# Two groups of four heads in one PSUM bank, at two column offsets of V, in both attentions of a two-layer network

## The chip, the cores and the metric

The kernel runs on one core of one Trainium2 chip, as one program for the whole network. The metric is the device time of one execution in microseconds (us). The kernel before took 1137.66 us (median of three).

## What is computed

The input is x of shape 8 x 512 x 128 in float32: eight batches of 512 tokens. Four blocks follow one another, each with its residual and a layer norm:

```
x = layernorm(x + attention0(x))   # 16 heads of 8 dims, softmax(q k^T / sqrt(128)) v
x = layernorm(x + moe(x))          # router, 32 experts, top 6, and a shared expert
x = layernorm(x + attention1(x))   # rms norms, rotary q and k, sigmoid(q k^T / sqrt(8)),
                                   #   each row divided by its sum, then an output product
x = layernorm(x + ffn(x))          # silu(gate) * up, 384 hidden
```

The change touches the two attentions alone: the product of the weights with V, and the division by the row sums.

## The kernel before

**Layout.** P is 128, a batch (b, of NB = 8) has T = 512 tokens in NT = 4 tiles of 128. The 16 heads have HD = 8 dims and form NG = 4 groups of HG = 4 heads. A batch is walked in NU = 32 units u. In unit u TensorE (PE) makes two matmuls of transposed scores (`s2`, L528 in attention 0, L1217 in attention 1) into one of two PSUM buffers `ps_s`, and ScalarE (ACT) turns them into `prob` by one activation of 128 x 1024 elements (L404, L1162). In each odd unit follows `pv` (L541, L1230): four matmuls, one for each head of the group, which add the product with V into the bank `ps_o`. Head j of a group takes PSUM partitions 32j to 32j+31 (CT = 32). Its stationary operand is 32 columns of V: 8 of V, a column of ones (which yields the row sum) and 23 columns of zeros. A group is complete after four `pv`, that is eight units.

**After each group.** ACT copies the bank `ps_o` to `osb` (`take_o`, L376 in attention 0, where one of the two buffers is called moe_dsb; L1150 in attention 1), after which PE may start the next group. PE then turns it by four transposes (`turn_o`, L549, L1245), so that tokens lie on partitions, and VectorE (DVE) makes the reciprocals of the row sums and multiplies (`divide`: L614 and L617; in attention 1 first an addition, L1362, then L1364 and L1367). Four copies, four times four transposes and four divisions stand in a batch of either attention. The four results fill `att`, which then gets x added and is normalised.

**Attention 0** also needs the maximum of each score row for the softmax. For that PE makes the untransposed scores in 64 matmuls a batch (`s1`, L463), one for each n from 0 to 63, and DVE reduces each to a maximum (`reduce_max`, L605, TENSOR_REDUCE of 128 x 512). Two n belong to each unit. These tiles rotate through FB = 3 PSUM banks `ps_f`, and so do the guests: the products for q, k and v, the two turned sets of maxima (`max0`, `max1`) and the turned outputs o0 to o3. The list `TURNS` holds all of them in order, each guest before the n that `GUEST_AT` gives it (o0, o1, o2, o3 before n = 29, 46, 62, 9), and `BANK` gives turn number i the bank i % 3. `free_bank` makes PE wait until the turn that last used the bank has been read: by DVE for an n or an o, by ACT for q, k, v, max0 and max1. Three turns lie between two uses of a bank, except where the list starts again: with 73 turns the turn of n = 0 has bank 0, and so has the last one, n = 63, directly before it. The stretch that is reduced at n = 8 to 63 belongs to the next batch.

**Attention 1** has no maxima. Its PE also makes, between the units, the transposes and products for a later batch (`front_use` at units 18, 20, 22, 24, 26, 28: L1200, then L1204 to L1206), V of the next batch (unit 2, L1183), and for the batch before the transposes of `att` (`turn_all`, unit 6, L1252), the output product (`project`, unit 8, L1259) and the transposes of x (`turn_x_next`, unit 15, L1268). `turn_o` stands at units 4, 12, 20 and 28, `take_o` at units 1, 9, 17 and 25. DVE runs `divide` at 4, 12, 20 and 28, and in unit 20 right after it the two passes L1330 and L1332, for whose result (`xrl`) the products of unit 22 wait.

**Order.** Each engine's order is written by hand in its function `units`, called by `walk`; the middle six batches run in a loop of two batches a pass. The last division of each attention is done in the first steps of the stage that follows (`FirstOutput`, `LastOutput`).

## Time and profile before

| | us |
|---|---|
| median of three runs | 1137.66 |
| lowest and highest | 1135.06 and 1138.14 |
| the profiled execution's own time | 1139.23 |
| span of its instructions in the trace | 1137.4 |
| attention 0, start of the first to start of the last softmax pass | 62 to 449 |
| mixture of experts | 454 to 757 |
| attention 1, start of the first to start of the last sigmoid | 760 to 1059 |

The profiled execution is 1.57 us longer than the median. Its span is the time from the first to the last instruction, 1.8 us less than its time. In the rows below, a row of the timeline stands for one or several like instructions in succession, and gives what ended the engine's idle time before them where there was any. "PEld" is the loading of the stationary operand, which overlaps PE's matmuls. A duration in a group of such instructions is that of one; the engine often starts the next before the one ends, so that the distance between two starts is what an instruction costs its engine.

### The profile page before, as it was taken

What the parts mean: (1) busy time and instruction counts of PE and PEld (TensorE: products, weight loads), DVE (VectorE), ACT (ScalarE), POOL (GpSimd) and SP (SyncE); (2) the same over time, 40 slices, a digit from 0 to 9 for tenths busy, and PEclk for the clock granted to TensorE, in tenths of its full rate; (3) what the DMA queues carried; (4) which work ended last, traced back from release to release, by engine and by line L of the source; (5) the groups of instructions that cost most, each with busy time, mean ns of one, the idle gap of its engine ahead of it and who ended that gap; (6) DMA issues with size and microseconds to landing.
All of it is one profiled execution on the core that took longest, in us unless ns stands there. A gap on an engine that the chain in (4) does not pass through costs nothing. (4 is left out here: it accounts for less than half of the span.)

```text
span 1137.4 us, 20713 instructions
## 1 busy us (share of the span) xinstructions
PE 1049.2 (92%) x5936; PEld 497.3 (44%) x5936; DVE 819.1 (72%) x1919; ACT 753.4 (66%) x977; POOL 458.5 (40%) x464
## 2 busy tenths in 40 slices
PE   3989999999999798999999999989999999999796
PEld 1112222222222133788888887753333333322484
DVE  4878999999999884887888788855445544534466
ACT  0057777777777577555555555557888888899553
POOL 0313224132242432666777677664333133300265
PEclk9999999999999899999999999999999999999898
DMA  4463122231222000443324332533421233120011
GB/s 149 134 211 96 51 77 80 66 96 44 79 79 57 1 3 4 148 141 118 95 100 148 125 107 90 161 101 98 125 89 53 82 111 95 43 84 1 1 29 46
DMA packets 74078, 97.16 MB, mean 85 GB/s; under 512 B 12701, under 2 KB 42269, under 8 KB 73629
## 3 DMA queue, kind: packets, MB, share of 16 engines
q1 hardware_dynamic: 74024, 96.51, 27.2%
q8 instruction: 26, 0.43, 0.2%
q14 instruction: 28, 0.22, 0.1%
HBM read 68.29 MB, written 27.79 MB: 84 GB/s over the span
## 5 line engine op out<-in xcount | busy, mean ns | idle before, releaser
L605 DVE TENSOR_REDUCE a_nmax<-a_ps_f 128x1 f32<-128x512 f32 x512 | 322.3, 683 | 46.5 <-PE a_ps_f L463 43.0
L404 ACT ACTIVATE a_prob<-a_ps_s 128x1024 f32<-128x1024 f32 x256 | 252.7, 1023 | 93.3 <-PE a_ps_s L528 91.7
L1162 ACT ACTIVATE a_prob<-a_ps_s 128x1024 f32<-128x1024 f32 x256 | 249.0, 1033 | 37.9 <-PE a_ps_s L1217 35.1
L1990 POOL TENSOR_TENSOR moe_hl<-moe_hid,moe_hh 128x512 fp32r<-128x512 f32 x136 | 175.8, 1298 | 93.1 <-ACT moe_hh L1880 93.1
L463 PE MATMUL a_ps_f<-a_ks,a_qs 48*128 48x512 bf16 x512 | 178.1, 417 | 35.2 <-DVE a_nmax L605 16.1
L1870 ACT ACTIVATE moe_ps<-moe_ps 128x512 f32<-128x512 f32 x128 | 74.5, 582 | 118.8 <-PE moe_ps L1800 118.1
L463 PEld LDWEIGHTS a_ps_f<-a_ks,a_qs 48*128 48x128 bf16 x512 | 40.3, 94 | 239.6 <-DVE a_nmax L605 197.7
L541 PE MATMUL a_ps_o<-a_prob,a_va 128*32 128x512 f32 x1024 | 138.8, 615 | 0.1
L1230 PE MATMUL a_ps_o<-a_prob,a_va 128*32 128x512 f32 x1024 | 136.4, 605 | 2.5 <-ACT a_osb L1150 1.3
L528 PE MATMUL a_ps_s<-a_qs,a_ks 51*128 51x512 bf16 x512 | 135.3, 390 | 1.5 <-ACT a_prob L404 1.5
L1920 DVE TENSOR_TENSOR moe_prod<-moe_cw,moe_ps 128x512 f32<-128x512 f32 x128 | 87.3, 682 | 32.1 <-PE moe_ps L1800 29.2
L1217 PE MATMUL a_ps_s<-a_qs,a_ks 48*128 48x512 bf16 x512 | 94.2, 385 | 8.1 <-ACT a_prob L1162 5.4
L212 POOL TENSOR_TENSOR a_parts<-a_qk,g_zero 128x512 bf16<-128x512 f32 x28 | 29.1, 1038 | 156.8 <-DVE a_qk L1343 60.9
L1929 DVE TENSOR_TENSOR moe_hid<-moe_prod,moe_ps 128x512 f32<-128x512 f32 x128 | 87.0, 679 | 6.8 <-DVE moe_prod L1920 2.4
L1880 ACT ACTIVATE moe_hh<-moe_hid 128x512 fp32r<-128x512 f32 x136 | 84.8, 625 | 4.1 <-DVE moe_hid L1929 4.0
L1217 PEld LDWEIGHTS a_ps_s<-a_qs,a_ks 48*128 48x128 bf16 x512 | 23.6, 92 | 128.4 <-ACT a_prob L1162 81.5
L661 POOL TENSOR_TENSOR a_msplit<-a_nmax,g_zero 128x32 bf16<-128x32 f32 x16 | 3.8, 238 | 166.2 <-DVE a_nmax L605 166.2
L1798 PE MATMUL moe_ps<-moe_xh,moe_whig 128*128 (+1 forms) x136 | 55.7, 409 | 1.7 <-DVE moe_hid L1929 1.7
L1820 PE MATMUL moe_ps<-moe_hl,moe_whid 128*128 128x512 f32 x136 | 54.1, 398 | 0.8 <-POOL moe_hl L1990 0.8
L1817 PE MATMUL moe_ps<-moe_hh,moe_whid 128*128 128x512 f32 x136 | 54.1, 398 | 0.3 <-ACT moe_dsb L1888 0.3
L1799 PE MATMUL moe_ps<-moe_xh,moe_wlou 128*128 (+1 forms) x136 | 54.2, 398 | 0.0
L174 POOL TENSOR_TENSOR a_ve<-a_mv,g_eps 128x4 f32<-128x4 f32 x16 | 3.2, 201 | 126.4 <-DVE a_mv L146 126.4
(282 smaller groups left out, 1734.5 us busy)
## 6 DMA issues: line engine op xcount, KB each, us to landing
moe_cw<-r_weights SPq DMA_DIRECT2D x256, 128.0 KB, 2.9
parts_q<-a_parts SPq DMA_DIRECT2D x48, 256.0 KB, 2.5
parts_k<-a_parts SPq DMA_DIRECT2D x48, 256.0 KB, 2.5
a_qs<-parts_q SPq DMA_DIRECT2D x128, 96.0 KB, 2.4
a_ks<-parts_k SPq DMA_DIRECT2D x128, 96.0 KB, 2.5
a_xt<-in_x_t SPq DMA_DIRECT2D x8, 256.0 KB, 2.9
out_x<-g_X SPq DMA_DIRECT2D x8, 256.0 KB, 2.3
moe_wg<-in_wg SPq DMA_DIRECT2D x1, 1088.0 KB, 6.4
```

The costliest lines, as they stand in the source:

```text
L404: nc.scalar.activation(prob[:, u % PSLOTS, :, :], ps_s[:, u % 2, :, :], ACT.Exp, scale=float(P) ** -0.5).then_inc(exp_done, 1)
L463: nc.tensor.matmul(ps_f[:, bank, :], stack_rows(qs[p], h, QKR)[:, qt * P:(qt + 1) * P], stack_rows(ks[p], h, QKR), start=True, stop=True). ...
L528: mm = nc.tensor.matmul(ps_s[:, u % 2, i, :], stack_rows(ks[p], h, MXR)[:, kt * P:(kt + 1) * P], stack_rows(qs[p], h, MXR), start=True, st ...
L541: mm = nc.tensor.matmul(ps_o[j * CT:(j + 1) * CT, :], va[p][:, kt, grp * HG + j, :], prob[:, (2 * e + j // UN) % PSLOTS, j % UN, :], start ...
L605: nc.vector.tensor_reduce(nmax[:, half_no, h % 2, col:col + 1], ps_f[:, bank, :], AX.X, ALU.max, negate=True).then_inc(max_done, 1)
L1162: nc.scalar.activation(prob[:, u % PSLOTS, :, :], ps_s[:, u % 2, :, :], ACT.Sigmoid, scale=float(HD) ** -0.5).then_inc(exp_done, 1)
L1217: mm = nc.tensor.matmul(ps_s[:, u % 2, i, :], stack_rows(ks[p], h, QKR)[:, kt * P:(kt + 1) * P], stack_rows(qs[p], h, QKR), start=True, st ...
L1230: mm = nc.tensor.matmul(ps_o[j * CT:(j + 1) * CT, :], va[p][:, kt, grp * HG + j, :], prob[:, (2 * e + j // UN) % PSLOTS, j % UN, :], start ...
L1880: nc.scalar.activation(hh[:, part_at(j), :], hid[:, hid_at(j), :], ACT.Copy).then_inc(hh_done, 1)
L1920: nc.vector.tensor_tensor(prod[:, bank(j), :], cw[:, j % RC, :], ps_u[:, bank(j), :], ALU.mult).then_inc(prod_done, 1)
L1929: nc.vector.tensor_tensor(hid[:, hid_at(j), :], prod[:, bank(j), :], ps_g[:, bank(j), :], ALU.mult).then_inc(hid_done, 1)
L1990: nc.gpsimd.tensor_tensor(hl[:, part_at(j), :], hid[:, hid_at(j), :], hh[:, part_at(j), :], ALU.subtract).then_inc(hl_done, 1)
```

## The change

Two groups now share the bank `ps_o`. `PER_O` = 2 groups make one output, `NO` = 2 outputs a batch, and `SLOT` = 16 is the distance between the two groups on the partitions of a head. The buffer `va` gets 16 columns of zeros at its front. For the first group of a pair the 32 stationary columns start at the head's own place (8 of V, ones, zeros), for the second they start 16 columns earlier (16 zeros, then 8 of V, ones, zeros). The rows 32j to 32j+15 of the bank thus hold a head of the first group, the rows 32j+16 to 32j+31 one of the second, and each adds zeros to the other. The accumulation starts at every eighth `pv` and stops seven later.

The core of the diff:

```diff
-OT_AT = (29, 46, 62, 9)
+OT_AT = (46, 9)
...
+def v_of_head(flat, kt, h):
+
+    at = (kt * H + h) * CT + SLOT * (h // HG % PER_O == 0)
+    return flat[:, at:at + CT]
...
+def output_parts(ps):
+
+    return ps.rearrange("p (k j q c) -> p k j q c", k=NT, j=HG, q=PER_O)
...
+def divide_outputs(nc, att, n, o, rec, done):
+
+    to, spread = outputs_of(att, n), [P, NT, HG, HD]
+    for q in range(PER_O):
+        ins = nc.vector.tensor_tensor(to[:, :, :, q, :], o[:, :, :, q, 0:HD],
+                                      rec[:, :, :, q].unsqueeze(3).broadcast_to(spread), ALU.mult)
+    ins.then_inc(done, 1)
...
-                        if second and u % 8 == 1 and (back if u > 8 else tail):
-                            take_o(*((b, u // 8 - 1) if u > 8 else (b - 1, NG - 1)))
+                        if second and u % 16 == 1 and (back if u > 16 else tail):
+                            take_o(*((b, u // 16 - 1) if u > 16 else (b - 1, NO - 1)))
...
-                if kt == 0:
-                    pe.wait_ge(o_taken, NG * b + grp + O_C)
+                if e % (PER_O * NT) == 0:
+                    pe.wait_ge(o_taken, NO * b + grp // PER_O + O_C)
...
-                                          start=(kt == 0), stop=(kt == NT - 1))
+                                          start=(e % (PER_O * NT) == 0), stop=((e + 1) % (PER_O * NT) == 0))
...
-                nc.vector.memset(va[i][:, :, :, HD + 1:CT], 0.0).then_inc(cleared, 1)
-                nc.vector.memset(va[i][:, :, :, HD:HD + 1], 1.0).then_inc(cleared, 1)
+                nc.vector.memset(v_tiles(va[i])[:, :, :, HD + 1:CT], 0.0)
+                nc.vector.memset(va[i][:, 0:SLOT], 0.0).then_inc(cleared, 1)
+                nc.vector.memset(v_tiles(va[i])[:, :, :, HD:HD + 1], 1.0).then_inc(cleared, 1)
...
-                    if u % 8 == TURN_AT and (back if u > 8 else tail):
-                        turn_o(*((b, u // 8 - 1) if u > 8 else (b - 1, NG - 1)))
+                    if u % 16 == TURN_AT and (back if u > 16 else tail):
+                        turn_o(*((b, u // 16 - 1) if u > 16 else (b - 1, NO - 1)))
```

So the copies at units 9 and 25, the transposes and divisions at units 12 and 28 (attention 1) and the guests before n = 29 and n = 62 (attention 0) are gone; those at units 1 and 17, 4 and 20, n = 46 and n = 9 stay where they were. The list of turns has 71 entries: n = 0 now follows the last user of its bank, n = 62, by two places, n = 1 follows n = 63 by two, and n = 2 follows n = 61 by five. Everywhere else three turns lie between two uses, as before. In attention 1 the transposes of x (unit 15) now wait for `y_taken`, the sum read by DVE at unit 8, instead of the first division of the batch. `turn_o` for the pair at unit 20 waits for `x_parted`, as the second group did before.

What stands on DVE in attention 0, from the first `divide` of the batch before the last to the first steps of the last batch; this part is written out without a loop. Before (L605 is `reduce_max`, L614 and L617 are `divide`):

```order
L605 TENSOR_REDUCE a_nmax<-a_ps_f 128x1 x5
L614 RECIPROCAL a_rec<-a_ps_f 128x16
L617 TENSOR_TENSOR moe_y<-a_ps_f,a_rec 128x4x32
L605 TENSOR_REDUCE a_nmax<-a_ps_f 128x1 x17
L614 RECIPROCAL a_rec<-a_ps_f 128x16
L617 TENSOR_TENSOR moe_y<-a_ps_f,a_rec 128x4x32
L605 TENSOR_REDUCE a_nmax<-a_ps_f 128x1 x16
L614 RECIPROCAL a_rec<-a_ps_f 128x16
L617 TENSOR_TENSOR moe_y<-a_ps_f,a_rec 128x4x32
L605 TENSOR_REDUCE a_nmax<-a_ps_f 128x1 x10
```

and now (L641 is `reduce_max`, L650 the reciprocal, L208 the two products):

```order
L641 TENSOR_REDUCE a_nmax<-a_ps_f 128x1 x22
L650 RECIPROCAL a_rec<-a_ps_f 128x32
L208 TENSOR_TENSOR moe_y<-a_ps_f,a_rec 128x4x32 x2
L641 TENSOR_REDUCE a_nmax<-a_ps_f 128x1 x26
L650 RECIPROCAL a_rec<-a_ps_f 128x32
```

The first and the third division are gone, the two that stay have a reciprocal of twice the elements and two products of the old size.

On ACT at the end of attention 1, from the copy for the batch before the last to the last one; L1162 is the sigmoid, L1150 `take_o`. Before:

```order
L1150 ACTIVATE a_osb<-a_ps_o 128x512
L1162 ACTIVATE a_prob<-a_ps_s 128x1024 x8
L1150 ACTIVATE a_osb<-a_ps_o 128x512
L1162 ACTIVATE a_prob<-a_ps_s 128x1024 x8
L1150 ACTIVATE a_osb<-a_ps_o 128x512
L1162 ACTIVATE a_prob<-a_ps_s 128x1024 x6
L1150 ACTIVATE a_osb<-a_ps_o 128x512
```

and now (L1193 is the sigmoid, L1181 the copy):

```order
L1181 ACTIVATE a_osb<-a_ps_o 128x512
L1193 ACTIVATE a_prob<-a_ps_s 128x1024 x16
L1181 ACTIVATE a_osb<-a_ps_o 128x512
L1193 ACTIVATE a_prob<-a_ps_s 128x1024 x14
L1181 ACTIVATE a_osb<-a_ps_o 128x512
```

Every second copy is gone, and sixteen sigmoids stand between two copies.

On DVE at unit 20 of attention 1, in the loop (L1350 scales x, L1391 to L208 are `divide`, L1359 and L1361 make the two halves of the scaled x for the products of unit 22), now:

```order
L1350 TENSOR_TENSOR a_xr<-a_xb,a_rr 128x512
L1390 ISA
L1391 TENSOR_SCALAR a_rec<-a_ps_t 128x32
L1392 ISA
L1393 RECIPROCAL a_rec<-a_rec 128x32
L1394 REGISTER_ALU
L208 TENSOR_TENSOR a_att<-a_ps_t,a_rec 128x4x32 x2
L1354 REGISTER_ALU
L1359 CAST a_xrh<-a_ps_f 128x512
L1361 TENSOR_TENSOR a_xrl<-a_ps_f,a_xrh 128x512
```

The order is that of before; the division ahead of the two passes has become longer.

## Rows read from the trace of the kernel before

**Rows 1.** Windows: us, busy time of each engine, PEclk, DMA share and GB/s
```profile
106.00:350.00 244.00, 232.01 (x1477) 63.47 (x1469) 225.80 (x436) 183.49 (x212) 65.81 (x95) 1.00 0.25 75
818.80:1042.90 224.10, 214.75 (x1490) 72.85 (x1487) 102.01 (x273) 197.98 (x217) 56.32 (x57) 1.00 0.23 71
```

**Rows 2.** Timeline of DVE, attention 0: start, us, instruction, [idle before, releaser]
```profile
197.38 0.25 DVE L614 RECIPROCAL a_rec<-a_ps_f 128x16 f32<-128x16 f32 x1
197.66 0.29 DVE L617 TENSOR_TENSOR moe_y<-a_ps_f,a_rec 128x128 f32<-128x128 f32 x1
197.87 3.44 DVE L605 TENSOR_REDUCE a_nmax<-a_ps_f 128x1 f32<-128x512 f32 x5
201.94 6.86 DVE L605 TENSOR_REDUCE a_nmax<-a_ps_f 128x1 f32<-128x512 f32 x11 [0.62 <-PE a_ps_f L463]
...
211.16 4.27 DVE L605 TENSOR_REDUCE a_nmax<-a_ps_f 128x1 f32<-128x512 f32 x7 [0.48 <-PE a_ps_f L463]
```

**Rows 3.** Timeline of DVE, attention 0: after `max1`, and three batches on
```profile
218.71 3.18 DVE L605 TENSOR_REDUCE a_nmax<-a_ps_f 128x1 f32<-128x512 f32 x5 [0.29 <-PE a_ps_f L463]
...
339.79 0.25 DVE L614 RECIPROCAL a_rec<-a_ps_f 128x16 f32<-128x16 f32 x1
```

**Rows 4.** Groups by line: count, busy us, mean ns, idle before and releaser
```profile
L614 DVE RECIPROCAL a_rec<-a_ps_f 128x16 f32<-128x16 f32 x31 | 7.7, 249 | 3.0 <-PE a_ps_f L549 2.8
L1625 DVE RECIPROCAL r_score<-r_e 128x128 f32<-128x128 f32 x8 | 7.5, 941 | 0.0
```

**Rows 5.** Timeline of PE, attention 0, before n = 0
```profile
208.57 1.06 PE L541 MATMUL a_ps_o<-a_prob,a_va 128*32 128x512 f32 x8
...
210.74 0.39 PE L463 MATMUL a_ps_f<-a_ks,a_qs 48*128 48x512 bf16 x2 [0.57 <-DVE a_nmax L605]
```

**Rows 6.** Weight loads of L1268: duration ns min, median, max, first and last start
```profile
L1268 PEld LDWEIGHTS a_ps_t<-g_ident,a_xb x28: 138/140/143, 818.8 to 1042.9; 128*128 128x128 f32 x28
```

**Rows 7.** Timeline of ACT, attention 1, one batch
```profile
927.39 0.60 ACT L1150 ACTIVATE a_osb<-a_ps_o 128x512 f32<-128x512 f32 x1
927.88 5.83 ACT L1162 ACTIVATE a_prob<-a_ps_s 128x1024 f32<-128x1024 f32 x6
934.13 1.94 ACT L1162 ACTIVATE a_prob<-a_ps_s 128x1024 f32<-128x1024 f32 x2 [0.42 <-PE a_ps_s L1217]
...
949.22 1.02 ACT L1162 ACTIVATE a_prob<-a_ps_s 128x1024 f32<-128x1024 f32 x1 [0.37 <-PE a_ps_s L1217]
```

**Rows 8.** Timeline of PE, attention 1, the same batch
```profile
922.62 0.66 PE L1252 MATMUL a_ps_t<-g_ident,a_att 128*128 128x128 f32 x4
...
928.04 1.07 PE L1230 MATMUL a_ps_o<-a_prob,a_va 128*32 128x512 f32 x8 [0.18 <-ACT a_osb L1150]
...
929.36 0.66 PE L1245 MATMUL a_ps_t<-g_ident,a_osb 128*128 128x128 f32 x4
929.94 0.39 PE L1217 MATMUL a_ps_s<-a_qs,a_ks 48*128 48x512 bf16 x2
...
941.41 0.50 PE L1204 MATMUL a_ps_f<-a_xrh,a_wh 128*128 128x512 f32 x1
```

**Rows 9.** Timeline of DVE, attention 1: divisions at units 4 and 20
```profile
921.57 0.29 DVE L1367 TENSOR_TENSOR a_att<-a_ps_t,a_rec 128x128 f32<-128x128 f32 x1
...
939.04 0.17 DVE L1362 TENSOR_SCALAR a_rec<-a_ps_t 128x16 f32<-128x16 f32 x1
...
940.60 0.69 DVE L1332 TENSOR_TENSOR a_xrl<-a_ps_f,a_xrh 128x512 fp32r<-128x512 f32 x1
```

**Rows 10.** Timeline of ACT, last batch of attention 1
```profile
1045.97 7.61 ACT L1162 ACTIVATE a_prob<-a_ps_s 128x1024 f32<-128x1024 f32 x8
```

**Rows 11.** Timeline of DVE, start of the kernel
```profile
4.35 0.11 DVE L597 MEMSET a_va<- 128x64 f32 x1
```

**Rows 12.** Windows at the one stall of PE in attention 0
```profile
369.50:377.00 7.50, 0.48 (x3) 0.00 (x0) 7.50 (x6) 1.02 (x1) 5.91 (x2) 0.73 0.00 0
377.00:382.00 5.00, 4.74 (x19) 0.91 (x20) 3.35 (x7) 1.26 (x2) 0.00 (x0) 0.50 0.00 0
```

**Rows 13.** Timeline of PE right behind that stall
```profile
378.83 1.93 PE L541 MATMUL a_ps_o<-a_prob,a_va 128*32 128x512 f32 x8
```

More of the change, by code:

```diff
@@ L24 @@
 CT = P // HG
+PER_O = 2
+NO = NG // PER_O
+SLOT = CT // PER_O
 PARTS = 3
@@ L1163, in units @@
                                              scale=float(HD) ** -0.5).then_inc(exp_done, 1)
-                    if u % 8 == 1 and (back if u > 8 else tail):
-                        take_o(*((b, u // 8 - 1) if u > 8 else (b - 1, NG - 1)))
+                    if u % 16 == 1 and (back if u > 16 else tail):
+                        take_o(*((b, u // 16 - 1) if u > 16 else (b - 1, NO - 1)))
             act.sem_inc(exp_done, EXP_C)
@@ L1409, in units @@
                         take_v(b + 1, 1 - p)
-                    if u % 8 == TURN_AT and (back if u > 8 else tail):
-                        divide(*((b, u // 8 - 1) if u > 8 else (b - 1, NG - 1)))
+                    if u % 16 == TURN_AT and (back if u > 16 else tail):
+                        divide(*((b, u // 16 - 1) if u > 16 else (b - 1, NO - 1)))
                     if back and is_last(b) and u in FFN_W_AT:
@@ L1493, in tensor @@
         if k == 1:
-            pe.wait_ge(self.att_done, NG * NB + 1)
+            pe.wait_ge(self.att_done, NO * NB + 1)
             for kt in range(NT):
```

173 lines of the change are left out of this document (84 added, 89 removed).

## The prediction

> **What bounds the kernel now.** I read the windows first, over a steady stretch of each attention. In attention 0 DVE is busy for 225.8 of 244 us, and ACT for 183.5; in attention 1 ACT is busy for 198.0 of 224.1 us and DVE for only 102.0 [rows 1]. PE shows 232.0 and 214.8 us, but a busy PE is modelled, so the timelines must decide. In attention 0 they say DVE: eleven reductions in 6.86 us stand without a gap, 0.62 us each, and what gaps there are end with an `s1` tile of PE [rows 2]. A batch lasts (339.79 - 197.38) / 3 = 47.5 us [rows 2, 3], and its 64 reductions take some 40 of them. In attention 1 a batch lasts (1042.9 - 818.8) / 6 = 37.35 us [rows 6], with two modes inside it. Where PE has only units to do, ACT runs six sigmoids in a row in 5.83 us [rows 7]: ACT bounds. Where PE has transposes or products in between, ACT waits 0.37 to 0.42 us for the scores [rows 7]: PE bounds. So three engines have to be followed, and the same edit is worth something else in each place. The mixture of experts and the last stage contain nothing of the change but its two heads.
>
> **Attention 0, per batch.** (a) Two of four divisions go. One costs DVE the time from 197.38 to 197.87, 0.49 us [rows 2], and DVE is the bound: 2 x 0.49 = 0.98 gained. The transposes that go with them (PE) and the copies (ACT) lie beside it and count nothing more. (b) The two that stay get longer. The reciprocal has 32 elements instead of 16: between 16 elements in 249 ns and 128 in 941 ns the slope is (941 - 249) / 112 = 6.2 ns [rows 4], so 0.10 us more. There is one more product, 0.21 us from start to start (197.66 to 197.87) [rows 2]. Together 0.31, twice: 0.62 lost. (c) But behind both stand gaps in which DVE waits for PE: 0.62 us behind the one at n = 46 [rows 2], and 0.29 behind the one at n = 9 [rows 3]. PE goes on while DVE divides longer, so part of the 0.62 falls into them. The bounds are 0 (PE is held by the three banks and gains no lead) and 0.62 (PE uses all of it, the second gap lacking 0.02); I take the middle, 0.3. (d) The list starts again without a bank that is used twice in succession. Before, PE waits 0.57 us for the reduction of n = 63 before it may make n = 0 [rows 5], and DVE then idles 0.48 [rows 2]. With two places between them, PE can make n = 0 while DVE reduces n = 63, which takes 0.62 and so is longer than the 0.48 of the round trip. But PE is still held at n = 1 until n = 63 is done, and the `pv` behind it (1.06 us, eight passes for its four matmuls [rows 5]) then comes later; a short gap may stand behind that. Bounds 0 and 0.48, I take 0.3, nearer to the full row since the round trip itself is hidden. Sum: 0.98 - 0.62 + 0.3 + 0.3 = 0.96 us a batch; from 0.36 to 1.46. Seven batches run with reductions and divisions together: 6.7 us (2.5 to 10.2).
>
> The last batch of attention 0 has no reductions; DVE, PE and ACT take turns there over the router's first steps. Two divisions go and one gets longer, 0.98 - 0.31 = 0.67 if all lies on the path, 0 if none. With PE's and ACT's parts the upper end is 1.2. I take 0.5.
>
> [...]
>
> **Attention 1, per batch.** (e) The copy at unit 9 stands in the stretch that ACT bounds: it costs from 927.39 to 927.88, 0.49 us [rows 7]. The `turn_o` that goes with it (unit 12) is hidden there, since PE waits for ACT anyway. (f) The copy at unit 25 and the `turn_o` of unit 28 stand where PE bounds: the transposes cost PE from 929.36 to 929.94, 0.58 us [rows 8], and ACT waits 0.37 behind such places [rows 7]; its copy is then free. Together 1.07. PE also waited 0.18 for the copy before the first `pv` of a group [rows 8]; that is the same time as the copy's and is counted only as an upper end, 1.25. (g) The division at unit 20 gets longer by 0.31, and by 0.02 for the addition over 32 elements. Behind it on DVE stand the two passes that make `xrl`, and for that PE's products of unit 22 wait: `xrl` ends at 941.29, and PE starts them at 941.41 [rows 8, 9], so there is 0.12 of slack and some latency; the delay is 0.2 to 0.33 where the division is the late one, and 0 where PE's own transposes of unit 20 are. I take 0.25 lost. (h) The division at unit 4 also gets longer, and `turn_all` waits for it: it ended at 921.86 and the transposes began at 922.62 [rows 8, 9], 0.76 us later. 0.33 fits in: nothing. Without that cover it would cost up to 0.33. (i) The new wait of unit 15 is for the sum of unit 8, which DVE made long before: nothing. Net 1.07 - 0.25 = 0.82 a batch; from 0.4 to 1.25. Seven batches: 5.7 us (2.8 to 8.7). The last batch has no fronts, ACT runs eight sigmoids in a row [rows 10], and two copies of 0.49 go: 1.0 (0.5 to 1.0).
>
> **Once only.** Two more short memsets on DVE at the start, each under the 0.11 of a 64-column one [rows 11], two on GpSimd, and 0.31 more in either head of the following stage, where PE and ACT have other work. I take 0.3 lost (0 to 0.8). No DMA is added, moved or passed; the matmuls of `pv` keep their number, shape and partitions, and read the same count of columns.
>
> **The sum.** 6.7 + 0.5 + 5.7 + 1.0 - 0.3 = 13.6 us, with ends of 5 and 21. The profiled execution took 1139.23, so a like one takes 1125.6; the median is 1.57 lower than it, 1137.66, so the forecast is **1124.0 us**.
>
> **The rivals.**
> *A, the new waits take most of it.* PE gains no lead in (c), the two short distances of (d) cost as much as the one they replace, and (g) costs its full 0.33 while DVE's and PE's parts in (e) and (f) only half show. Then attention 0 gives 0.36 x 7 = 2.5 and attention 1 0.4 x 7 + 0.5 = 3.3: about 6 us, 1131.7. For it speaks that gaps of 0.62 and 0.29 come from PE's bursts, which the change does not touch; against it, that the wait of 0.57 in rows 5 plainly hangs on a bank that the change frees. 0.16.
> *B, more is gained.* In attention 0 PE is nearly as full as DVE. With two transposing turns less PE gets 2 x 0.58 us of lead, and gaps behind the k product and `max0` (0.62 each) shrink; in attention 1 everything of (e) and (f) counts. Attention 0 gives 1.5 x 7, attention 1 1.15 x 7 + 1: 19 us, 1118.5. 0.16.
> [...]
> *D, within measurement of no change.* The time goes into waits that the rows do not show, of ACT for `pv` or of DVE for transposes: 1137.7. 0.04.
>
> **How the numbers follow.** The forecast has 0.60, A and B 0.16 each, C and D 0.04 each. The predicted time is the forecast's. From 1116 to 1133 the range takes in nearly all of the forecast's ends and most of A and B, and leaves out C and D. About 0.3%, or 3.4 us, is what a measurement of this kernel can tell from no change. Faster by more than that: the forecast, B, and nearly all of A, 0.89. Within it: D and the tail of A, 0.07. Slower: C, 0.04.
>
> **What would show it.** In the trace after: the idle 0.48 before n = 0 gone or under 0.2, batches of attention 0 of 46.5 us, a division of 0.80 us from start to the next reduction, a reciprocal of about 0.35 us. In attention 1 batches of 36.5 us, six or more sigmoids in a row without a copy, and `xrl` later than PE's wish for it by 0.2 or so at unit 22. PEclk of 1.00 in both stretches. The forecast is wrong if the batches of attention 0 stay at 47.1 or above, if PE idles before L1204 for more than 0.4, or if a granted clock under 1.00 shows in the steady stretches.

## The result, and the profile after

The changed kernel takes **1121.5 us** (median of four, 1118.78 to 1123.58), the kernel before 1137.9 in the same comparison. The ratio is 0.9854 with a 95% interval of 0.983 to 0.9878, so 13.9 to 19.3 us are gained. The forecast was 1124.0 in a range of 1116 to 1133. It held, but the sum is better than its terms: those of attention 0 and of the start were too small, those of attention 1 too large, and one stage that gained, the mixture of experts, stood nowhere in the sum. That these errors cancel is luck.

The profiled execution took 1123.58 us against 1139.23. The landmarks in both traces, in us:

| stretch | before | after | difference | forecast |
|---|---|---|---|---|
| start to the first exponential | 62.2 | 60.8 | -1.4 | +0.3 |
| attention 0, first to last exponential | 386.8 | 376.8 | -10.0 | -7.2 |
| from there to the first sigmoid of attention 1 | 311.4 | 309.9 | -1.5 | 0 |
| attention 1, first to last sigmoid | 298.3 | 295.4 | -2.9 | -6.7 |
| from there to the end | 78.7 | 78.6 | -0.1 | 0 |

Two of these differences hold more than the change. Attention 1 of the kernel before takes 298.3 us here, but 299.3 in two kernels of the experiments with the same code for it (e1, e6). At its start the clock's record differs: before, PEclk is 1.00 from 458 to 1062 us, and after there is a stretch at 0.50 from 746.0 to 752.9. Here is PE from 746 to 753 us in the changed kernel and then in e12, which has the same attention 1 and no such stretch:

```profile
746.00:753.00 7.00, 6.14 (x26) 0.51 0.28 85
```

```profile
746.00:753.00 7.00, 5.53 (x40) 1.00 0.28 85
```

Between kernels that agree in this, attention 1 gains 3.9 us both ways: 299.3 (e1) to 295.4 (after) with the stretch at 0.50, 298.3 (before) to 294.3 (e12) without it. So 2.9 is too low for the change by 1.0. The other difference is that of the mixture of experts; it is taken up under "Sixty-four bytes".

**The steady stretches.** First the windows, with the columns of [rows 1] (PE, PEld, DVE, ACT, POOL, PEclk, DMA share, GB/s), then the weight loads that answer to [rows 6] and the group that answers to [rows 4].

```profile
120.00:350.00 230.00, 219.08 (x1390) 58.66 (x1382) 216.95 (x413) 173.00 (x196) 65.47 (x94) 1.00 0.25 75
806.00:1028.00 222.00, 209.92 (x1446) 68.08 (x1444) 98.68 (x249) 192.71 (x205) 56.36 (x57) 1.00 0.23 71
```

```profile
L1297 PEld LDWEIGHTS a_ps_t<-g_ident,a_xb x28: 137/141/143, 806.3 to 1027.7; 128*128 128x128 f32 x28
```

```profile
L650 DVE RECIPROCAL a_rec<-a_ps_f 128x32 f32<-128x32 f32 x12 | 4.2, 348 | 0.0
```

The granted clock is 1.00 in both stretches. The reciprocal of 32 elements takes 348 ns; that of 16 took 249 [rows 4], so 99 ns more, as worked out: it lies on the line through 16 and 128 elements (249 + 16 x 6.18 = 348).

**Attention 0 on DVE**, one batch (the timeline that answers to [rows 2] and [rows 3]):

```profile
146.69 0.35 DVE L650 RECIPROCAL a_rec<-a_ps_f 128x32 f32<-128x32 f32 x1
147.07 0.49 DVE L208 TENSOR_TENSOR moe_y<-a_ps_f,a_rec 128x128 f32<-128x128 f32 x2
147.47 3.14 DVE L641 TENSOR_REDUCE a_nmax<-a_ps_f 128x1 f32<-128x512 f32 x5
151.24 9.95 DVE L641 TENSOR_REDUCE a_nmax<-a_ps_f 128x1 f32<-128x512 f32 x16 [0.62 <-PE a_ps_f L498]
161.48 3.78 DVE L641 TENSOR_REDUCE a_nmax<-a_ps_f 128x1 f32<-128x512 f32 x6 [0.30 <-PE a_ps_f L498]
165.17 0.35 DVE L650 RECIPROCAL a_rec<-a_ps_f 128x32 f32<-128x32 f32 x1
165.56 0.49 DVE L208 TENSOR_TENSOR moe_y<-a_ps_f,a_rec 128x128 f32<-128x128 f32 x2
165.96 4.46 DVE L641 TENSOR_REDUCE a_nmax<-a_ps_f 128x1 f32<-128x512 f32 x7
...
192.84 0.35 DVE L650 RECIPROCAL a_rec<-a_ps_f 128x32 f32<-128x32 f32 x1
```

From 146.69 to 192.84 a batch takes 46.15 us; the next ones alternate between 46.07 and 46.15, mean 46.11. Before it was 47.47. Segment by segment:

- From the division at n = 46 to the end of the wait behind it: 197.38 to 201.94 before, 4.56 us [rows 2]; 146.69 to 151.24 now, 4.55. The division is 0.29 longer and nothing came later: the five reductions behind it took 3.44 us [rows 2] and now take 3.14. They had short waits between them (the second began 0.11 us after the first had ended), and these are filled. The wait of 0.62 behind them is the same.
- From there to the division at n = 9 there are 22 reductions. Before, with a division and the 0.48 us of wait [rows 2], they took 201.94 to 216.65, 14.71 us; now 151.24 to 165.17, 13.93. The division is 0.49 of the 0.78. The wait of 0.48 before n = 0 is gone, but one of 0.30 has come a few turns later.
- Behind n = 9 the wait of 0.29 [rows 3] is gone: seven reductions follow without a gap. It has taken up the longer division.
- In the rest of the batch the fourth division went, 0.49. The wait before n = 26 is 0.43 where it was 0.34.

The four make 1.3 us. The pair of batches shown is a short one before and a long one after; by the means, a batch gains 1.36 to 1.38.

The wait of 0.30 comes from one of PE for a bank. PE may make n = 1 only when n = 63, two turns earlier in the same bank, has been reduced, and behind n = 1 and n = 2 stands a `pv`, so that n = 3 is late (timeline of PE, at n = 1):

```profile
159.45 0.39 PE L498 MATMUL a_ps_f<-a_ks,a_qs 48*128 48x512 bf16 x1 [0.31 <-DVE a_nmax L641]
```

**Attention 1 on ACT**, the batch that answers to [rows 7]:

```profile
912.74 1.02 ACT L1193 ACTIVATE a_prob<-a_ps_s 128x1024 f32<-128x1024 f32 x1 [0.31 <-PE a_ps_s L1248]
914.14 5.76 ACT L1193 ACTIVATE a_prob<-a_ps_s 128x1024 f32<-128x1024 f32 x6 [0.37 <-PE a_ps_s L1248]
920.38 1.94 ACT L1193 ACTIVATE a_prob<-a_ps_s 128x1024 f32<-128x1024 f32 x2 [0.49 <-PE a_ps_s L1248]
...
926.46 1.02 ACT L1193 ACTIVATE a_prob<-a_ps_s 128x1024 f32<-128x1024 f32 x1 [0.90 <-PE a_ps_s L1248]
927.86 1.02 ACT L1193 ACTIVATE a_prob<-a_ps_s 128x1024 f32<-128x1024 f32 x1 [0.37 <-PE a_ps_s L1248]
929.11 1.02 ACT L1193 ACTIVATE a_prob<-a_ps_s 128x1024 f32<-128x1024 f32 x1 [0.23 <-PE a_ps_s L1248]
```

The six sigmoids at 914.14 have no copy before them any more, but a wait of 0.37 us in its place. The sigmoid ahead of them is 912.74 now and 926.37 in the trace of before, 13.63 us apart; the six start at 914.14 and 927.88 [rows 7], 13.74 apart. The copy of 0.49 was worth 0.11. At 929.11 stands a wait of 0.23 that was not there.

PE shows why, in the same batch:

```profile
911.22 1.16 PE L1288 MATMUL a_ps_t<-a_w,a_att_t 128*128 128x128 f32 x8
912.31 0.39 PE L1248 MATMUL a_ps_s<-a_qs,a_ks 48*128 48x512 bf16 x2
912.63 1.07 PE L1261 MATMUL a_ps_o<-a_prob,a_va 128*32 128x512 f32 x8
913.63 0.61 PE L1248 MATMUL a_ps_s<-a_qs,a_ks 48*128 48x512 bf16 x4
```

The output product of unit 8 (L1288, 1.16 us) and a `pv` make the scores of unit 10 late; ACT would have waited for them without the copy too. The copy stood in a PE-bound place, one unit ahead of the ACT-bound stretch for which the prediction took it.

The turn at unit 28 that went cost PE 0.41 us, from 949.03 to 949.44, not the 0.58 of unit 12 in [rows 8]: here a matmul of products follows it, there the scores (timeline of PE, kernel before):

```profile
949.03 0.65 PE L1245 MATMUL a_ps_t<-g_ident,a_osb 128*128 128x128 f32 x4
949.44 0.48 PE L1204 MATMUL a_ps_f<-a_xrh,a_wh 128*128 128x512 f32 x1
```

From there to the next single pair of scores before and after drift apart by 0.38. In all: 0.11 + 0.38, less 0.11 at unit 22 (below), 0.38 a batch. A steady batch fell from 38.05 to 37.67 us. The mean of six intervals fell from 37.35 to 36.9 (806.3 to 1027.7), but one of the six, from unit 15 of the seventh batch to unit 15 of the last, has no fronts: 33.5, now 32.75.

**The start.** The timeline of DVE, before and then after, at the split of the first k:

```profile
12.17 0.43 DVE L211 CAST a_parts<-a_qk 128x512 bf16<-128x512 f32 x1 [0.48 <-ACT a_qk L376]
```

```profile
11.39 0.42 DVE L245 CAST a_parts<-a_qk 128x512 bf16<-128x512 f32 x1
```

With 73 turns q and k had the same bank, 0, and PE waited 2.05 us at the start until ACT had copied q. With 71 turns k has bank 2. The wait of 0.48 is gone. Over all runs with a trace, the first exponential starts at 62.2 to 62.3 us in the four kernels in which q and k share a bank, and at 60.6 to 61.3 in the ten in which they do not. The start of the first reduction (22.95 before, 22.25 now, but 22.8 in e1 and e12) also hangs on a DMA, that of the parts of k: ahead of its first scores PE waits for it 10.8 us in the kernel before, 12.7 in the changed one, 13.4 in e1 and 13.1 in e12. No run changed the bank of k alone.

### The profile page after: what moved, and what is told of

Its sections match the earlier page's. It is cut to its first block and busy times, and to the rows that moved or that the text cites. A ratio compares the mean times of both kernels' runs of the same rounds, so it can differ in the third digit from the quotient of the medians.

```text
span 1121.5 us, 20149 instructions
## 1 busy us (share of the span) xinstructions
PE 1032.1 (92%) x5808; PEld 485.4 (43%) x5808; DVE 811.5 (72%) x1873; ACT 737.4 (66%) x945; POOL 458.8 (41%) x466
## 5 line engine op out<-in xcount | busy, mean ns | idle before, releaser
L641 DVE TENSOR_REDUCE a_nmax<-a_ps_f 128x1 f32<-128x512 f32 x512 | 320.0, 684 | 41.0 <-PE a_ps_f L498 40.1
L1193 ACT ACTIVATE a_prob<-a_ps_s 128x1024 f32<-128x1024 f32 x256 | 248.9, 1029 | 42.9 <-PE a_ps_s L1248 40.0
L1895 ACT ACTIVATE moe_ps<-moe_ps 128x512 f32<-128x512 f32 x128 | 74.5, 582 | 117.4 <-PE moe_ps L1825 116.7
L1823 PE MATMUL moe_ps<-moe_xh,moe_whiu 128*128 (+1 forms) x136 | 54.0, 397 | 0.0
L1824 PE MATMUL moe_ps<-moe_xh,moe_wlog 128*128 (+1 forms) x136 | 53.8, 396 | 0.0
```

Source lines behind the costliest of these rows:

```text
L641: nc.vector.tensor_reduce(nmax[:, half_no, h % 2, col:col + 1], ps_f[:, bank, :], AX.X, ALU.max, negate=True).then_inc(max_done, 1)
L1193: nc.scalar.activation(prob[:, u % PSLOTS, :, :], ps_s[:, u % 2, :, :], ACT.Sigmoid, scale=float(HD) ** -0.5).then_inc(exp_done, 1)
L1823: nc.tensor.matmul(dst, w[0][:, j, :], hi, start=True, stop=False)
```

## The experiments

The times are medians, each beside runs of the kernel before on the same chip; a batch of attention 0 is the mean of two neighbours, one of attention 1 is a steady one, and the mixture of experts (MoE) is read from the first to the last of its 128 sigmoids on ACT (L1870, L1895), in the profiled execution.

| kernel | us | ratio, 95% interval | att. 0 batch | att. 1 batch | MoE |
|---|---|---|---|---|---|
| before | 1137.9 | 1 | 47.49 | 38.05 | 293.9 |
| after | 1121.5 | 0.9854 (0.983 to 0.9878) | 46.11 | 37.67 | 291.4 |
| e1, attention 0 alone | 1125.49 | 0.9878 (0.9852 to 0.9904) | 46.11 | 38.05 | 291.3 |
| e2, attention 1 alone | 1130.0 | 0.9923 (0.9904 to 0.9942) | 47.48 | 37.64 | 291.1 |
| e3b, +0.4 on DVE at n = 46 | 1122.17 | 0.9866 (0.9845 to 0.9887) | 46.11 | 37.67 | 292.5 |
| e4b, +0.4 on DVE at n = 9 | 1121.34 | 0.985 (0.9828 to 0.9871) | 46.38 | 37.67 | 292.7 |
| e5, after, 72 places | 1120.13 | 0.9835 (0.9813 to 0.9857) | 45.99 | 37.67 | 292.5 |
| e6, before, 74 places | 1136.67 | 0.9985 (0.9973 to 0.9997) | 47.48 | 38.05 | 293.9 |
| e7, copy at unit 9 | 1122.26 | 0.9864 (0.985 to 0.9879) | 46.10 | 37.69 | 291.6 |
| e9, division behind xrl | 1120.85 | 0.9845 (0.9823 to 0.9868) | 46.11 | 37.56 | 291.6 |
| e10, before, buffers 64 bytes lower | 1135.12 | 0.9966 (0.9955 to 0.9977) | 47.48 | 38.06 | 290.7 |
| e11, three findings together | 1118.14 | 0.9827 (0.9813 to 0.9842) | 45.99 | 37.50 | 291.7 |
| e12, after, MoE buffers back | 1121.92 | 0.9849 (0.9836 to 0.9861) | 46.11 | 37.67 | 291.1 |
| e13, e11 with banks from n = 16 | 1121.51 | 0.985 (0.9837 to 0.9863) | 46.11 | 37.50 | 292.5 |

The times differ less than their intervals for most pairs. The batches in the traces repeat to 0.02 us between kernels that share the code, so small terms are read from them. Spans of a whole stage do not: the MoE varies by 1.4 us between kernels with the same placement and the same code for it.

### Each attention alone

In e1 the function `attention1` and the class `LastOutput` are those of before, and the rest is as changed; in e2 it is the reverse, with the shift of the top buffers in both:

```diff
-        wide = nc.sbuf_usable_end // 32 * 32 - 2 * NB * T * 4
+        wide = nc.sbuf_usable_end // 32 * 32 - 2 * NB * T * 4 - SLOT * 4
```

> The change in attention 0 alone; attention 1 and its head as before. Theory T (read from the two traces): attention 0 gives 1.3 us in each of seven batches and about 2 more in its first and last, so 11 to 12 us: about 1126.5 against 1137.9, and batches of attention 1 stay at 37.35. Rival F (the split of the forecast): attention 0 gives 7.2, so about 1130.7. Rival N: the gains of the two attentions do not add, since less work in one changes what the other meets; then this and the kernel with the change in attention 1 alone sum to something other than 16.4.

> The change in attention 1 alone; attention 0 as before. Theory T: 0.45 us in each of seven batches and 0.5 to 1 in the last, so 3 to 4.5 us: about 1134, batches of attention 0 at 47.45, of attention 1 at 36.9. Rival F: 6.7 us, about 1131.2. With the kernel that changes attention 0 alone the gains sum to 15 to 17 us by T.

e1 gains 12.8 us by the medians, nearer to theory T than to the 7.2 of the forecast's split; its attention 0 takes 376.0 us, 10.8 less than before. e2 gains 8.3, far more than the 3 to 4.5 of T. But its trace shows only 3.9 of it in attention 1 (294.4 instead of 298.3 us from the first to the last sigmoid). Another 2.8 lie between the attentions, in the MoE, where neither change does anything. The two gains sum to 21.1, and the whole change gives 16.4. The intervals of the three are wide (some 3, 2 and 3 us to either side), but the traces say the same: something is in both halves and counts once. That is rival N in its outcome, though not by its reason, and it led to e10.

### A longer division

The edit of e3b (of e4b with `n == 1`, the division at n = 9):

```diff
                 divide_outputs(nc, att, n, o, rec, att_done)
+                if n == 0:
+                    nc.vector.memset(pad[:, :], 0.0)
```

> The changed kernel, with a memset of 400 columns of an unused tile on DVE behind the division at n = 46 of attention 0: about 0.4 us more of DVE work there in each of eight batches. Theory T: DVE's longer work there runs beside a burst of PE that sets the next reduction but four; DVE still waits 0.62 us behind it, that wait shrinks to 0.2 and batches stay at 46.15 (at most 0.1 longer, under 1 us in all). Rival D: the banks hold PE back as DVE is late, and the 0.4 counts in full: batches of 46.55, about 3 us more.

> The same behind the division at n = 9, where the changed kernel leaves no wait of DVE. Theory T: the change has used up the wait of 0.29 us there, so the 0.4 counts until the next wait for PE that no bank causes: 0.2 to 0.4 in each of seven batches, 1.5 to 2.9 us. Rival P: PE alone sets the length of a batch, the wait of 0.43 us behind n = 26 takes the 0.4, and the time moves by under 0.5 us.

The timeline of DVE in e3b, behind n = 46:

```profile
147.55 0.39 DVE L655 MEMSET a_pad<- 128x400 f32 x1
147.86 3.01 DVE L642 TENSOR_REDUCE a_nmax<-a_ps_f 128x1 f32<-128x512 f32 x5
151.20 9.94 DVE L642 TENSOR_REDUCE a_nmax<-a_ps_f 128x1 f32<-128x512 f32 x16 [0.33 <-PE a_ps_f L499]
```

The memset delays the five reductions by 0.43 us, the wait of 0.62 shrinks to 0.33, and the batch stays at 46.11. Theory T holds, rival D falls. In e4b a batch is 0.27 longer (46.38): between the ends that T gave, and not rival P. So the two places differ. Behind n = 46 DVE still waits for PE after the change, and 0.4 us more fits in. Behind n = 9 the change had used up the wait, and only 0.16 of the 0.43 still fits between the seven reductions, which take 4.30 instead of 4.46. The times cannot tell these differences; the batches do.

### The banks

The edit of e5 and of e6 is the same line:

```diff
-BANK = {t: i % FB for i, t in enumerate(TURNS)}
+BANK = {t: (i + (i >= TURNS.index(21))) % FB for i, t in enumerate(TURNS)}
```

> The changed kernel, with the three banks of attention 0 numbered one further from turn n = 21 on, so that the list has 72 places and starts again with each bank three turns old; the two short distances (two turns) now stand at n = 21 and 22, where DVE writes four products of the normalisation, 1.11 us, between two reductions. Theory T: the gap of 0.30 us some turns after the start of the list comes from the two-turn distances there and goes; nothing comes back at n = 21, since PE makes the two tiles beside the 1.11 us; batches of attention 0 go from 46.1 to 45.85, 2 us in all, about 1119.5. Rival P: that gap comes from PE's own burst of a pv and transposes and stays; the time does not move (within 0.5 us a run), or the gap only moves.

> The kernel before with nothing changed but the numbering of the banks, one further from n = 21 on: the list has 74 places, and it starts again with two turns between uses of a bank, as in the changed kernel, where it was one. Theory T (term (d) of the prediction, measured alone): the wait of PE of 0.57 us before n = 0 and DVE's 0.48 behind it go, 0.30 stay; a batch of attention 0 gets 0.2 to 0.35 shorter, 47.45 to 47.15, 2 us in all, about 1136. Rival P: the wait is only handed on to the next burst, and nothing is gained (47.4).

The timeline of DVE in e6, from the division at n = 62 on:

```profile
207.36 3.28 DVE L605 TENSOR_REDUCE a_nmax<-a_ps_f 128x1 f32<-128x512 f32 x5
210.94 3.77 DVE L605 TENSOR_REDUCE a_nmax<-a_ps_f 128x1 f32<-128x512 f32 x6 [0.30 <-PE a_ps_f L463]
...
227.55 1.89 DVE L605 TENSOR_REDUCE a_nmax<-a_ps_f 128x1 f32<-128x512 f32 x3 [0.57 <-PE a_ps_f L463]
```

Where the list starts again the wait of 0.48 is replaced by one of 0.30, as in the changed kernel. The eleven reductions from 207.36 to 214.63 take 7.27 us, and took 7.45 (209.20 to 216.65) before: 0.18 gained. But before n = 26 the wait is 0.57 where it was 0.34, since the short distances at n = 21 and 22 hold PE ahead of the q product. The batch is the same, 47.48. Rival P describes it: the wait was handed on, here by my own edit. The price of term (d) alone is thus 0.18 us where the list starts again; over a batch this edit shows nothing of it. The time of e6 is 0.15% below that of before (0.03 to 0.27%), about 1.7 us; of that the last batch of attention 0 holds 0.26 us (41.53 to 41.27), the steady ones nothing, and where the rest lies stays open.

In e5 the wait of 0.30 goes (22 reductions in a row) and the one before n = 26 grows from 0.43 to 0.57:

```profile
149.90 13.72 DVE L641 TENSOR_REDUCE a_nmax<-a_ps_f 128x1 f32<-128x512 f32 x22 [0.62 <-PE a_ps_f L498]
...
176.46 1.89 DVE L641 TENSOR_REDUCE a_nmax<-a_ps_f 128x1 f32<-128x512 f32 x3 [0.57 <-PE a_ps_f L498]
```

T had the cause of the 0.30 right, and was wrong that the short distances cost nothing at n = 21. Net 0.12 a batch, half of what T gave, and 0.8 us in seven batches.

### The copy of unit 9

```diff
+                    if u == 9 and tail:
+                        act.wait_ge(ot_done, NO * b + OT_C)
+                        nc.scalar.activation(osb[:, 1, :], osb[:, 1, :], ACT.Copy)
```

> The changed kernel with a copy on ScalarE (ACT) of a 128x512 tile put back at unit 9 of attention 1 in seven batches, without the transposes and the division that went with it (it copies a tile onto itself). Theory T: the copy stands in a wait of 0.37 us of ACT for the scores, which comes from the product with W_o that PE makes at unit 8; it costs 0.12 us a batch, under 1 us in all (a batch 36.9 to 37.0). Rival F (term (e) of the prediction): ACT is the bound there and the copy costs 0.49 us a batch, 3.4 us in all (37.4).

The timeline of ACT in e7, around unit 9:

```profile
913.48 1.02 ACT L1193 ACTIVATE a_prob<-a_ps_s 128x1024 f32<-128x1024 f32 x1 [0.31 <-PE a_ps_s L1251]
914.40 0.62 ACT L1199 ACTIVATE a_osb<-a_osb 128x512 f32<-128x512 f32 x1
914.92 5.75 ACT L1193 ACTIVATE a_prob<-a_ps_s 128x1024 f32<-128x1024 f32 x6
```

The copy takes the place of the wait of 0.37, and the six sigmoids start 1.44 us behind the one before them instead of 1.40. A batch is 0.02 to 0.04 longer, attention 1 in all 0.3 us. Theory T holds with an even lower price; term (e) of the prediction, 0.49, falls.

### The division ahead of xrl

The edit of e9 moves the division of unit 20 in DVE's program:

```diff
-                    if u % 16 == TURN_AT and (back if u > 16 else tail):
-                        divide(*((b, u // 16 - 1) if u > 16 else (b - 1, NO - 1)))
+                    if u == TURN_AT and tail:
+                        divide(b - 1, NO - 1)
...
                     if u in FRONT_AT and qk_on:
                         take_front(b + 2, p, FRONT_AT.index(u))
+                    if u == 16 + TURN_AT and back:
+                        divide(b, 0)
```

> The changed kernel, with the division of unit 20 of attention 1 placed behind the two passes that make xrh and xrl on DVE, not ahead of them. Theory T (term (g) measured): xrl is made 0.2 us earlier against PE's transposes, PE's products of unit 22 no longer wait for it, and the wait of ACT of 0.23 us behind them goes: 0.1 to 0.2 us a batch, about 1 us in all (a batch 36.75; xrl ends at least 0.15 us earlier after the transposes than in the changed kernel). Rival F (the size in the prediction): 0.25 a batch and 1.8 us. Rival X: PE's transposes of unit 20 are what is late, since they wait 0.58 us for xr, and nothing moves (36.9).

The timeline of ACT behind it has no wait of 0.23 any more:

```profile
927.57 1.02 ACT L1193 ACTIVATE a_prob<-a_ps_s 128x1024 f32<-128x1024 f32 x1 [0.90 <-PE a_ps_s L1248]
928.97 2.17 ACT L1193 ACTIVATE a_prob<-a_ps_s 128x1024 f32<-128x1024 f32 x2 [0.37 <-PE a_ps_s L1248]
```

A batch takes 37.56 instead of 37.67: term (g) is 0.11 us, by removing it alone. T holds. Where the rest of the 0.33 went, the first of the two passes (`xrh`) shows, against PE's transposes of unit 20, before and then after:

```profile
939.18 0.66 PE L1200 MATMUL a_ps_f<-g_ident,a_xr 128*128 128x128 f32 x4 [0.58 <-DVE a_xr L1321]
...
939.88 0.69 DVE L1330 CAST a_xrh<-a_ps_f 128x512 fp32r<-128x512 f32 x1
```

```profile
925.44 0.65 PE L1231 MATMUL a_ps_f<-g_ident,a_xr 128*128 128x128 f32 x4 [0.58 <-DVE a_xr L1350]
...
926.32 0.68 DVE L1359 CAST a_xrh<-a_ps_f 128x512 fp32r<-128x512 f32 x1
```

Before, the pass began 0.04 us after the transposes had ended (939.84): they were the late ones, and not the division. Now it begins 0.18 later against them (0.88 us from their start instead of 0.70), so 0.15 of the 0.33 is hidden behind the transposes, and 0.06 of the rest in the slack before PE's products. The 0.7 us that this makes in all is less than the interval of the times.

### Sixty-four bytes

The row of V is 16 columns longer in the changed kernel, and to make room for it the buffers at the top of SBUF start 64 bytes lower. In the MoE those addresses hold `moe_xh` and `moe_xl`, the moving operands of six of nine products. The edit of e10, in the kernel before:

```diff
-        wide = nc.sbuf_usable_end // 32 * 32 - 2 * NB * T * 4
+        wide = nc.sbuf_usable_end // 32 * 32 - 2 * NB * T * 4 - 64
```

> The kernel before, with nothing changed but the place of the buffers at the top of SBUF, 64 bytes lower, as the change puts them; in the mixture of experts these are the moving operands of two thirds of the products. Theory S: the matmuls that read them are some ns shorter each, the stage's 128 units take 291.2 us from the first to the last sigmoid instead of 293.9, and the time falls by 2 to 4 us, to about 1135. It would explain why the gains of the two halves, 12.8 and 8.3, add up to more than the 16.8 of both. Rival I: the place of the instructions, not of the data, makes the difference, or chance does; then the stage stays at 293.9 and the time at 1137.9.

e12 is the changed kernel with the MoE's two buffers, and the first stacks of attention 1 that lie in the same place, put back:

```diff
-        e[name] = nc.alloc_sbuf_tensor_at("a1_" + name, [P, HH, T], BF16, offset=wide + i * NB * T * 4)
+        e[name] = nc.alloc_sbuf_tensor_at("a1_" + name, [P, HH, T], BF16, offset=wide + 64 + i * NB * T * 4)
...
-            m["xh"], m["xl"] = (nc.alloc_sbuf_tensor_at(f"moe_x{n}", [P, NB, T], F32R, offset=wide + i * NB * T * 4)
+            m["xh"], m["xl"] = (nc.alloc_sbuf_tensor_at(f"moe_x{n}", [P, NB, T], F32R, offset=wide + 64 + i * NB * T * 4)
```

> The changed kernel with the buffers at the top of SBUF that the mixture of experts reads (its two halves of x, and the first stacks of attention 1 that lie in the same place) put back 64 bytes, to where they were before; those of attention 0 stay 64 bytes lower. Theory S: the stage's products take some ns more each again, its 128 units take 293.9 us instead of 291.4, and the time rises by 2 to 3 us, to about 1124; both attentions stay as they are (46.1 us a batch, and 37.7). Rival O: the address that matters is another one (of attention 0's tiles or of what follows them), and nothing moves (291.5, 1121.5).

The first and last of the MoE's sigmoids (line, count, ns min/median/max, first and last start), in the order before, after, e10, e12:

```profile
L1870 ACT ACTIVATE moe_ps<-moe_ps x128: 582/582/591, 455.4 to 749.3; 128x512 f32<-128x512 f32 x128
```

```profile
L1895 ACT ACTIVATE moe_ps<-moe_ps x128: 582/582/593, 444.8 to 736.2; 128x512 f32<-128x512 f32 x128
```

```profile
L1870 ACT ACTIVATE moe_ps<-moe_ps x128: 582/582/591, 456.0 to 746.7; 128x512 f32<-128x512 f32 x128
```

```profile
L1895 ACT ACTIVATE moe_ps<-moe_ps x128: 582/582/590, 444.5 to 735.6; 128x512 f32<-128x512 f32 x128
```

e10 is 0.34% faster than the kernel before (0.23 to 0.45%), with not one instruction changed, and its MoE takes 290.7 us instead of 293.9. Not all of this is the placement. The first sixteen units of the stage take 36.8 to 38.1 us, and differ by up to 1.3 between kernels with the same code and the same placement; the clock's record falls to 0.50 for 3 to 7 us near their start in all traces but that of e12. From the 17th sigmoid to the last it is 256.1 us before and 253.5 in e10: the place of data matters by 2.5 us. Theory S as it stood falls with e12, though: with the MoE's buffers back where they were the stage does not return to 293.9 but takes 291.1. It is not the address of these buffers by itself.

Between the 17th and the 97th sigmoid, a stretch that repeats best, the fourteen traces show three levels: 182.33 and 182.46 (before, e6); 180.66, 180.67 and 180.85 (e10, e2, e12); 181.28 to 181.38 (all nine others). What fits all of them, as a reading made afterwards: the change also makes `rec` of attention 0 64 bytes larger, and what is allocated behind it, the MoE's weights among it, moves up by 64. The distance between weights and x is then the old one in the first level, 64 bytes less in the second (by the one shift or by the other), and 128 less in the third. That it is the distance was not tried by itself, and why it should matter stays open. From the 17th sigmoid to the last the same three groups take 255.9 to 256.1, 253.5 to 253.8 and 254.5 to 254.6 us, so that 1.4 us of the change's gain go with the placement. The products agree with the grouping: over the whole stage the mean of that of `moe_hh` with `moe_wlod` is 394 ns before and 395 in e6, 388 in e10 and in e2, 389 in e12, and 396 after. e2 and e10 differ in their instructions and agree in these numbers; before and e10 have the same instructions and do not. So rival I, the place of the instructions, falls. One of the 80 units between those sigmoids takes 182.46 / 80 = 2.281 us before and 2.258 in e10, 1% less.

### Three findings together

e11 has the banks of e5, the division of e9, and the scores of unit 21 ahead of the transposes of xr, for which PE waits 0.58 us:

```diff
+                    if u == FRONT_AT[1] + 1 and qk_on:
+                        front_use(b + 2, p, 1, front)
...
-                    if u in FRONT_AT and qk_on:
+                    if u in FRONT_AT and qk_on and u != FRONT_AT[1]:
                         front_use(b + 2, p, FRONT_AT.index(u), front)
```

> A version built from the findings: the changed kernel with the banks renumbered from n = 21 on, the division of unit 20 behind xrl, and PE's scores of unit 21 placed ahead of the transposes of xr, which wait 0.58 us for DVE. Theory T: 3.1 us from the banks (from the trace of the kernel with that alone), 1 from the division, and 0.32 us a batch (2.2 in all) from the scores that fill PE's wait: 6.3 less than the changed kernel, about 1115.2; batches of attention 0 45.7, of attention 1 36.4 to 36.5. Rival X: the scores made earlier gain nothing, since ACT is given its next tile by the same burst; then 1117.4 and 36.75 a batch. Rival Y: the xr chain then becomes later and the 0.3 is lost in unit 22: 1119.

e13 is e11 with `TURNS.index(16)` in place of `TURNS.index(21)`.

> The version with all three findings, with the banks renumbered from n = 16 on and not from n = 21: there DVE makes the statistics of the normalisation, 1.2 us, between two reductions, and five more reductions and the normalisation lie between it and the q product. Theory T: the 0.14 us that the short distances at n = 21 cost before n = 26 (a wait of 0.57 instead of 0.43) is not paid at n = 16, since PE has more of DVE's other work to catch up beside: batches of attention 0 45.8 to 45.85 instead of 46.0, 1 us less than the version with n = 21, about 1117. Rival P: v's product or its copy by ACT is late instead, a wait stands behind n = 16 or the 0.57 stays, and batches stay at 46.0 or are longer.

e11 has the lowest median of all, 1118.14. Its ratio to before, 0.9827, overlaps with that of the changed kernel, 0.9854. Its trace supports 1.9 us of the 3.4: 0.12 in each of seven batches and 0.17 in each of six. The scores moved ahead gave only 0.06 of their 0.32 a batch. The timeline of PE says why: the wait for xr is 0.26 instead of 0.58, but the products of unit 22 now wait 0.19 for xrl. That is most of rival Y; the xr chain sets the pace there, and filling PE's wait only shows the next one. T had also put the banks at 3.1 us, the difference of the whole spans of attention 0 in after and e5 (376.8 and 373.8); the batches hold 0.8 of it, and e11, with the same banks, takes 375.8. The rest did not repeat.

```profile
923.98 0.66 PE L1231 MATMUL a_ps_f<-g_ident,a_xr 128*128 128x128 f32 x4 [0.26 <-DVE a_xr L1352]
...
926.14 0.50 PE L1235 MATMUL a_ps_f<-a_xrh,a_wh 128*128 128x512 f32 x1 [0.19 <-DVE a_xrl L1363]
```

e13 puts the short distances at n = 16. The wait before n = 26 is 0.43 again, as T had it, but one of 0.33 stands five turns earlier, and a batch takes 46.11: rival P.

```profile
174.04 1.29 DVE L641 TENSOR_REDUCE a_nmax<-a_ps_f 128x1 f32<-128x512 f32 x2 [0.33 <-PE a_ps_f L498]
...
178.58 1.89 DVE L641 TENSOR_REDUCE a_nmax<-a_ps_f 128x1 f32<-128x512 f32 x3 [0.43 <-PE a_ps_f L498]
```

The change in the banks is worth 0.12 us a batch at n = 21 and nothing at n = 16. A list of 71 turns over three banks has to have its short distances somewhere.

## Why the prediction was right, and where it was not

**(a) Two divisions of 0.49 us gone, 0.98 a batch.** Right; each shows whole, since DVE bounds around them.

**(b) The longer division, 0.62 for both.** Right as a size: 0.78 to 0.79 us from start to next reduction, 0.80 forecast; the reciprocal 348 ns, 0.35 forecast.

**(c) Half of it falls into gaps, 0.3.** This step was sized wrongly: all of it did, 0.6, the upper bound that the prediction gave. It took the middle between the bounds, for want of a row that says whether PE gains a lead, and it looked for the room in the wrong place behind n = 46: the gap of 0.62 stayed as it was. The trace had the row: the five reductions behind n = 46 took 3.44 us [rows 2], 0.69 each, where eleven others took 0.62 each. Such excess is waiting in short pieces that the timeline does not print, and it went when the division got longer. e3b shows that even 0.43 us more would have been hidden.

**(d) The start of the list, 0.3.** The effect is there, with a short wait left behind it, as forecast. In the kernel before it is worth 0.18 (e6); in the changed one 0.29 of the 22 reductions' 0.78 is not the division's, of which this may be 0.18; the rest was not measured by itself.

Together attention 0 gains 1.36 to 1.38 a batch instead of 0.96. With its ends it gives 10.0 us against 7.2, inside the 11.4 of the upper ends. The five steady batches give 6.9 of the 10.0, the first 0.9, the seventh 1.2 and the last 0.95, where 0.5 was forecast. The difference is the step (c) in the main, and the last batch.

**(e) The copy at unit 9, 0.49.** Wrong: 0.02 to 0.11 (e7, and the two timelines). The prediction read the six sigmoids behind it [rows 7] as ACT-bound and counted the copy to them. It did not look at what the first of the six would have waited for. The product of unit 8, 1.16 us of PE, stands two rows above in PE's timeline.

**(f) The turn at unit 28, 0.58.** Right in kind, 0.38 in size. It was priced with the row of unit 12, where other work follows.

**(g) The longer division ahead of xrl, 0.25 lost.** Right in place, 0.11 in size (e9). The prediction named the case in which PE's transposes are the late one, at 0; that was the kernel before, and the division had to outgrow them first.

**(h), (i)** Nothing, as forecast: `turn_all` starts as far behind the scores as before, and no wait shows at unit 15.

So a batch of attention 1 gains 0.38 instead of 0.82, and attention 1 gains 3.9 where the clock's record agrees (2.9 between the two profiled runs) instead of 6.7, near the low end of 3.3. The prediction also counted (f) in seven batches, and only six have fronts behind them. From unit 16 of the seventh batch on, without fronts, 1.2 were gained (48.5 to 47.3), of which the last batch has 0.76, where 1.0 was forecast.

**Once only, 0.3 lost.** Wrong in sign: 1.4 gained. The line `if BANK["q"] == BANK["k"]` in PE's program was in the code, and 73 and 71 turns give k different banks. The prediction followed the banks only where the list starts again. That the bank is the cause is read from the traces, not from a run of its own.

**What no step had.** The MoE's 2.5 us (291.4 instead of 293.9), of which 1.4 go with the placement of data by the grouping above, and 1.0 lies in the first sixteen units, whose length varies between traces. The prediction said that this stage contains nothing of the change. It contains its addresses.

The errors cancel: 13.6 forecast, 15.9 between the two profiled spans, with +2.8 from attention 0, +1.7 from the start, +1.5 from the middle, and -3.8 from attention 1 (-2.8 at a like clock). Of the rivals, A was nearly right about attention 1 (3.3) and B about attention 0 (10.5), though not by B's reason: the gaps behind the k product and `max0` are as long as before, 0.34 and 0.62, and it was the longer divisions that fell into gaps. C, the slower one, and D did not occur; PEclk is 1.00 in both steady stretches, and the 0.50 of [rows 12], at which eight passes of `pv` took 1.93 us [rows 13] instead of 1.06 [rows 5], shows in neither.

## What to carry to other kernels

Before a removed instruction is counted as gained, look one row up on the engine that feeds its successor: a copy at the head of a stretch that its engine bounds can still stand in a wait for the stretch before, as the copy of 0.49 us at unit 9 did, which was worth 0.11. The five reductions behind n = 46 took 3.44 us where another five took 3.18 [rows 2, 3]: the excess was hidden waits, and the longer division fell into them for nothing (3.14 after the change). Such groups are worth looking for. When the length of a rotating list changes, work out the buffer of every entry, not just of the ones at the seam, and measure a shift of addresses by itself before crediting its gain to the edit that caused it. Compare stages of two traces only after comparing their clock records, and take small terms from stretches that repeat.

## What the runs showed of the hardware

**Placement of data in SBUF moved TensorE's pace by 1.0% in one stage.** With the same instructions and the buffers at the top of SBUF 64 bytes lower, 111 units of a stage in which PE is busy for 199.4 of 200 us took 253.5 us instead of 256.1, and the whole kernel 0.34% less (0.23 to 0.45%).

**PEclk read 1.00 in a window where PE took the durations of 0.50.** In the windows from 20 to 60 us (PE and PEclk, DMA share, GB/s) the kernel before shows 1.00 and the changed one 0.50:

```profile
20.00:60.00 40.00, 34.36 (x67) 1.00 0.52 151
```

```profile
20.00:60.00 40.00, 35.85 (x70) 0.50 0.51 154
```

But the same eight passes of the v product took the same time in both, nearly twice the 1.16 us that eight passes of the same line take at 126 us in the kernel before:

```profile
27.08 2.08 PE L448 MATMUL a_ps_f<-a_w,a_xt 128*128 128x128 f32 x8
```

```profile
26.38 2.08 PE L483 MATMUL a_ps_f<-a_w,a_xt 128*128 128x128 f32 x8
```

The author's reading of these durations is that PE ran at 0.50 in both. The trace of before holds no record of the clock ahead of 69 us, and the window above gives that stretch as 1.00; that of after has one, from 12 to 67 us at 0.50. By an estimate (55 us x 0.5 / 1121.5 us = 0.025) that makes most of the difference between a mean clock of 0.956 and one of 0.985, and it says nothing of the time: the four runs of the changed kernel have 0.956, 0.985, 0.957 and 0.986 at 1123.58, 1122.46, 1120.54 and 1118.78 us.

**Smaller differences of the mean clock went with the time in these runs.** Of the 49 runs of the kernel before that stand beside the experiments, the thirteen with a mean clock of 0.982 took 1138.55 to 1140.45 us, the seventeen with 0.985 took 1136.58 to 1138.31, and the four with 0.987 took 1134.91 to 1137.42.
